# Both layer normalisations of a Mamba-like layer with a mixture of experts, applied by ScalarE instead of VectorE

## The reference

```python
def _layernorm(x, axis=-1, eps=1e-05):
    m = jnp.mean(x, axis=axis, keepdims=True)
    v = jnp.var(x, axis=axis, keepdims=True)
    return (x - m) / jnp.sqrt(v + eps)

x = L0_attn_x
x = x + _L0_attn_ref(_layernorm(x), ...)   # projections, conv of 4 taps, damped oscillator per head, gate, output
x = x + _L0_ffn_ref(_layernorm(x), ...)    # router over 8 experts, the best 2, GELU experts, a shared expert
```

## Time and profile before

| | us |
|---|---|
| median of 3 runs | 580.45 |
| lowest and highest run | 577.06, 587.46 |
| the profiled execution | 578.51 |
| its span, from the first to the last instruction | 576.8 |

### The profile page before, as it was taken

The page is one execution under the profiler, slowest core; times in us unless marked ns, Lnnn a source line. Parts: engine busy times, 40 slices in busy tenths (PEclk is TensorE's granted clock), DMA queues, the critical chain, the costliest instruction groups (busy, mean ns, idle before and its releaser), DMA issues.

```text
span 576.8 us, 9365 instructions
## 1 busy us (share of the span) xinstructions
PE 435.0 (75%) x3240; PEld 352.0 (61%) x3240; DVE 486.3 (84%) x1206; ACT 275.1 (48%) x459; POOL 208.7 (36%) x269
## 2 busy tenths in 40 slices
PE   2942006997889929897989928897889929986997
PEld 1832005886756717785856717786756718875886
DVE  5389998989899998989799998979899997886342
ACT  1641233555646623455665624455646624334363
POOL 2021006767630007667620007657630007784000
PEclk9977557999989977999999969999989978999999
DMA  7400000000000010000000000000000000000000
GB/s 232 125 1 1 0 0 1 2 3 1 1 1 0 2 36 2 1 1 1 2 1 1 2 18 0 3 2 0 1 2 0 1 19 2 2 2 1 1 9 11
DMA packets 8433, 7.05 MB, mean 12 GB/s; under 512 B 1593, under 2 KB 7618, under 8 KB 8258
## 3 DMA queue, kind: packets, MB, share of 16 engines
q1 hardware_dynamic: 8386, 6.46, 3.7%
HBM read 5.41 MB, written 1.05 MB: 11 GB/s over the span
## 4 chain that ended last, share of the span: by engine, by line
DVE 24%; PE 22%; POOL 12%; issue 8%; ACT 3%; DVEq 0%; POOLq 0%; ACTq 0%
POOL vt L1493 4%; PE HB L514 4%; DVE tp L1102 3%; POOL big L1490 3%; DVE xr L1319 3%; PE HB L522 3%; DVE mm L1219 2%; PE RR L542 2%; PE OO L542 2%; DVE mm L1181 2%; DVE hist L1102 2%; POOL rinv L1510 2%; DVE pr L1181 2%; PE GV L542 2%; PE BC L560 1%
## 5 line engine op out<-in xcount | busy, mean ns | idle before, releaser
L1490 POOL TENSOR_TENSOR big<-mm 128x256 f32<-128x256 f32 x64 | 48.8, 763 | 258.1 <-DVE mm L1219 258.1
L560 PE MATMUL BC<-xnT,winT 128*128 128x128 f32 x512 | 76.4, 296 | 79.8 <-DVE mm L1219 79.7
L560 PEld LDWEIGHTS BC<-xnT,winT 128*128 128x128 f32 x512 | 67.6, 206 | 85.7 <-DVE mm L1219 82.2
L1493 POOL TENSOR_TENSOR vt<-mm 128x256 f32<-128x256 f32 x64 | 59.3, 927 | 0.0
L823 ACT ACTIVATE pr<-hist 128x512 f32<-128x512 f32 x32 | 34.0, 1115 | 52.2 <-DVE hist L1102 52.2
L514 PE MATMUL HB<-xnT,w 128*128 128x512 f32 x108 | 54.5, 631 | 2.5 <-ACT sqs L908 2.1
L845 ACT ACTIVATE big<-GV 128x256 f32<-128x256 f32 x64 | 24.6, 384 | 66.5 <-PE GV L584 65.5
L582 PE MATMUL GV<-big,vt 128*128 128x128 f32 x256 | 44.6, 299 | 11.6 <-POOL vt L1493 11.6
L1102 DVE TENSOR_TENSOR tp<-big,hist 128x256 f32<-128x256 f32 x124 | 51.8, 418 | 1.4
L1217 DVE TENSOR_TENSOR mm<-BC,pr 128x512 f32<-128x512 f32 x64 | 44.1, 688 | 4.9
L582 PEld LDWEIGHTS GV<-big,vt 128*128 128x128 f32 x256 | 36.0, 203 | 18.4 <-POOL vt L1493 15.9
(11 more groups left out here) (188 smaller groups left out, 1075.7 us busy)
## 6 DMA issues: line engine op xcount, KB each, us to landing
xr<-in_x SPq DMA_DIRECT2D x4, 256.0 KB, 4.8
winT<-in_w_inT SPq DMA_DIRECT2D x1, 1024.0 KB, 6.3
w<-in_rw SPq DMA_DIRECT2D x1, 1024.0 KB
out<-xr SPq DMA_DIRECT2D x3, 256.0 KB, 2.3
taps<-in_dw_wT SPq DMA_DIRECT2D x1, 512.0 KB, 3.7
w<-in_sw SPq DMA_DIRECT2D x2, 128.0 KB
out<-xr SPq DMA_DIRECT2D x2, 128.0 KB, 1.8
winT<-in_w_inT SPq DMA_DIRECT2D x1, 130.0 KB, 2.8
```

The source lines that it names most:

```text
L560: last = pe.matmul(b[:, j * TS:(j + 1) * TS], winT[:, col:col + NS], xt, start=True, stop=True)
L1490: pool.tensor_tensor(wt[q % 8][:], m[:, 0], m[:, 3], ALU.add)
L1493: pool.tensor_tensor(vt[q % 2][:], view(m, 5 * TS, (-3 * TS, 2), (1, TS)), view(m, 3 * TS, (TS, 2), (1, TS)), ALU.subtract).then_inc(wv_do ...
```

## The change

ScalarE applies both normalisations as Identity(scale * x + bias), with rstd as per-partition scale and a new tile `shift` = -mean * rstd as per-partition bias. VectorE makes `nmean` = -mean, one instruction more in each `norm_stats`; GpSimd makes `shift` from it after rstd, behind a wait of its own chain, and signals `ln_rstd` only then. `norm_apply` moves to ScalarE's queue: at the head behind the exponential of the parameters; LN1 in step 2, behind that step's `vt_copy`; LN2 behind the z of the next group and ahead of `norm2`; EARLY in step 15; LAST ahead of its `norm2`. Two waits are added for order that VectorE's queue gave before: `norm_stats` waits for the `ln_rstd` of the normalisation before it, and TensorE's first expert output of a whole group waits for the state sum of the group's last tile (`z_done`), since both use the bank RR.

```diff
@@ tensor, expert_out
+                if whole(u) and e == 0:
+                    pe.wait_ge(z_done, GT * (u + 1))
@@ scalar
+            def norm_apply(kind, u):
+                g, c0, c1 = UNITS[u] if kind == LN2 else (u, 0, GT)
+                n = ln_index(kind, u)
+                act.wait_ge(ln_rstd, n + 1)
...
+                if n:
+                    act.wait_ge(h_ready, USE[last] + 1)
+                for c in range(c0, c1):
+                    last = act.activation(xn[:, c, :], xr[g % 3][:, c, :], ACT.Identity, bias=shift[:, c:c + 1],
+                                          scale=rstd[:, c:c + 1])
+                last.then_inc(ln_xn, 1)
...
             act.activation(sgt[:, 2 * NH:4 * NH], sgt[:, 0:2 * NH], ACT.Exp, scale=-1.0).then_inc(prep_a, 1)
+            norm_apply(LN1, 0)
...
                     if g + 1 < NG:
+                        if k == F_XN:
+                            norm_apply(LN1, g + 1)
                         front_early(g + 1, k - 1)
...
                     else:
+                        if k == A_XN:
+                            norm_apply(LN2, EARLY)
...
                     front_late(g + 1, "z", 1)
+                    norm_apply(LN2, g)
                     norm2(g)
...
+            norm_apply(LN2, LAST)
             norm2(LAST)
@@ vector
+                if ln_index(kind, u):
+                    dve.wait_ge(ln_rstd, ln_index(kind, u))
                 for c in range(c0, c1):
                     last = dve.bn_aggr(mv[:, c, :], stats[:, c, :])
                 link(last)
+                dve.tensor_scalar(nmean[:, c0:c1], mv[:, c0:c1, 0], -1.0, None, ALU.mult)
                 dve.tensor_scalar(mv[:, c0:c1, 1], mv[:, c0:c1, 1], EPS_LN, None, ALU.add).then_inc(ln_var, 1)
-            def norm_apply(kind, u):
...
-                for c in range(c0, c1):
-                    last = dve.tensor_scalar(xn[:, c, :], xg[:, c, :], mv[:, c, 0:1], rstd[:, c:c + 1],
-                                             ALU.subtract, ALU.mult)
-                last.then_inc(ln_xn, 1)
...
                     matrices(g + 1, 0)
-                    norm_apply(LN2, g)
                     matrices(g + 1, 1)
@@ gpsimd, rstd_of
-                pool.tensor_tensor(rstd[:, c0:c1], mv[:, c0:c1, 1], mhalf[:, c0:c1], ALU.pow).then_inc(ln_rstd, 1)
+                link(pool.tensor_tensor(rstd[:, c0:c1], mv[:, c0:c1, 1], mhalf[:, c0:c1], ALU.pow))
+                pool.tensor_tensor(shift[:, c0:c1], nmean[:, c0:c1], rstd[:, c0:c1], ALU.mult).then_inc(ln_rstd, 1)
```

More of the change, by code:

```diff
@@ L143, in build @@
         rstd = sb("rstd", 128, GT)
+        shift = sb("shift", 128, GT)
+        nmean = sb("nmean", 128, GT)
         dtts = [sb(f"dtt{i}", 128, KP) for i in range(2)]
@@ L748, in _ @@
             by_tile = lambda t: t.rearrange("p (c t) -> p c t", c=GT)
+            def norm_apply(kind, u):
+                g, c0, c1 = UNITS[u] if kind == LN2 else (u, 0, GT)
+                n = ln_index(kind, u)
+                act.wait_ge(ln_rstd, n + 1)
+                if kind == LN2:
+                    last = ("xnT", u + 1) if whole(u) else ("xnT2", u - 1)
+                else:
+                    last = ("xnT2", g - 2) if g >= 2 else ("xnT", g - 1)
+                if n:
[4 more added lines that the diff above has]
+                last.then_inc(ln_xn, 1)
             def front_early(g, k):
@@ L1037, in front_early @@
                     norm_stats(LN1, g)
-                if k == F_XN:
-                    norm_apply(LN1, g)
                 if k == F_EXP:
@@ L1359, in _ @@
             dve.wait_ge(prep, 1)
-            front_early(0, F_XN)
             dve.wait_ge(ld_u, LD_U)
@@ L1411, in _ @@
                             norm_stats(LN2, EARLY)
-                        if k == A_XN:
-                            norm_apply(LN2, EARLY)
                         if k == A_ROUTER + 1:
@@ L1433, in _ @@
                     matrices(g + 1, 2)
-            norm_apply(LN2, LAST)
             for e in range(MID_STEPS - A_ADDS, NE - 1):
```

## The result

The changed kernel takes 587.75 us, median of 4 runs (586.04 to 589.87); the kernel before, over the same runs, 579.48 (577.06 to 587.46). The ratio is 1.0157, with a 95% interval of 1.0111 to 1.0202: slower by 1.1 to 2.0%, at the border of what this kernel's measurement tells from no change. The profiled execution took 588.24 us, its span 586.5, 9.7 more than before; mean granted clock 0.900 (before 0.911). In the program after, the rows are L767, shift L1469, nmean L1047, the added eps L1048, the square L860, z L829, the pair's first product L1212, the transposes L438, the router's product L501.

A forecast was written before the change was run, and what follows sets the result against it. VectorE was busiest (84%), but the normalised rows stood on the chain that ended last. LN1 1.6 + LN2 3.6 + head 0.6 + halves 0.1 and 0.8 = +6.7 us on 578.51: 585.2, median 586.0; own range 582 to 590, overall 579 to 593.

The forecast's parts named there:

- ScalarE's instruction: Each new 128-column normalising instruction on ScalarE: 0.48 us alone, one every 0.38 us in a row.
- shift: GpSimd's added tiny multiplication behind rstd: ScalarE is released 0.28 us after rstd.
- LN1: Three sites early in the groups: next pair's square queues behind the normalisation, 0.54 us each, +1.6 us.
- VectorE's relief counts: Rival: ScalarE's queue holds nothing wanted, so VectorE's freed time at LN1 and LN2 is won; about -12, 566 us; chance 0.07.
- LN2: Three sites between groups: rows behind z's copy on ScalarE make TensorE's transposes 1.19 us late each, +3.6 us.
- the third rival: At six LN1 and LN2 sites TensorE's clock falls to the 1.2 GHz level; 10 us on top, 595.4; chance 0.13.
- its sign for the third rival: Behind LN1 and LN2 sites: a granted clock below 0.95 would mean the third rival holds.
- Head: Start of the kernel: TensorE begins the transposes at 8.45 in place of 7.84, +0.6 us.
- Second half: Last group's second half: normalisation behind expert 7's GELU on ScalarE delays TensorE's transposes, +0.8 us.
- First half: Last group's first half: shift fits GpSimd's 0.55 us idle time or hangs out by up to 0.1, +0.1 us.
- Costed at nothing: Nine negated means on VectorE (1.8 us if uncovered), TensorE's new wait for the last state sum, and activation table loads: 0.
- Absorbed: Rival: delays inside groups go into VectorE's idle time; only head and second half remain, +1.4, 580.0; chance 0.14.

The follow-up runs named there:

- experiment 1: `ln1_later`: changed kernel with LN1's normalisation one step later in ScalarE's queue and its TensorE transposes a step later too; 583.38 us, ratio 1.0105.
- Experiments 6 and 7: Experiment 6 is `ln1_none`, ratio 0.9973; experiment 7 is `only_ln1_spread`, ratio 0.9974.
- `only_ln1_spread`: Kernel before with only LN1 of groups 1 to 3 on ScalarE, two rows behind each of two pairs; 577.6 us, ratio 0.9974.
- `rows_back_no_nmean`: Changed kernel with all 32 normalising instructions back on VectorE and the negated mean dropped, shift still made but unread; 579.86 us, one run.
- `ln1_none`: Kernel before with LN1 rows of groups 1 to 3 left out, ScalarE writing one column instead; negated mean and shift stay; 578.79 us, ratio 0.9973.

## Why the prediction was right, and where it was off

The range of 582 to 590 around the forecast of 586.0 holds the measured 587.75, and the result is a slower kernel within the border of 2%. The order in ScalarE's queue costs what was forecast, place by place. That the total fits as well as it does is in part luck: in the profile 6.7 us were forecast and 9.7 came, two terms were too small, and the 0.8 us added for the median rest on the three runs' 580.45, where later medians of the kernel before were 578.7 to 579.3. By its steps:

- *ScalarE's instruction*, 0.48 us and one per 0.38: measured 0.482, and 1.64 for four. *shift* 0.28 us behind rstd's end: 226.24 to 226.55, 0.31.
- *LN1*, 0.54 a site behind the square: 0.55 to 0.59, three times, in both profiles of the changed kernel. Shown by experiment 1, where the wait went with the order. The prediction was wrong about its premise, though: it held VectorE's 3.3 us at the site for the most that could be won, and against "VectorE's relief counts" it named only ScalarE's order. Experiments 6 and 7 show that with the order mended some 0.45 us a site is won and the other 2.8 are not there: the pairs behind wait for other engines' work.
- *LN2*, 1.19 a site: right where the clock holds (1.15 on the average of `ln1_later`'s three), but 2.0 and 2.3 on average in the two profiles of the changed kernel. The term is short by the router's product at the low clock and what follows it, 2.5 us over three sites in the first profile, 3.4 in the second. This is the mechanism of the third rival, which was given 0.13 as a case of its own with 10 us; it came as an addition of a few. The argument against it, that TensorE kept 1.00 around one hole of 1.80, was a single stretch, and it ends 0.36 us behind that hole; the trace has 1.00 from 274 to 280 us too, but the same rows showed 0.79 behind the other hole. What the prediction did not look at is the seam itself: in the kernel before the clock was already 0.66 behind two of the three LN2 sites. So its sign for the third rival, a clock below 0.95 there, was met (0.79 and 0.54) and could not tell: it holds without the change too. What counts is whether the fall comes ahead of the router's product.
- *Head* 0.6: 0.65, and 0.58 to 0.80 in the other profiles with it. *Second half* 0.8: 0.8 to 1.0 where the clock behind the last pair is as in the kernel before, and gone when the rows stand ahead of the GELU.
- *First half* 0.1: 0.62. The term looked only at whether shift fits into GpSimd's idle time. What cost was nmean, "costed at nothing" at LN1 and LN2 and not looked at here: it pushed the adding of eps behind the start of a 256-column sum of GpSimd.
- *Costed at nothing.* TensorE's new wait and the activation table: nothing in any trace. The negated means: nothing at LN1, as forecast (0.23, 0.26 and 0.24 with, 0.24, 0.26 and 0.24 without), but 0.16 at the head (0.30 with, 0.14 without, one profile each) and 0.6 at the first half, so 0.8 us.
- *Absorbed*, the rival at 0.14: no step of the table is taken back inside a group, but for the two stray stretches.

Added up, 0.65 + 1.70 + 3 x 1.19 + 0.62 + 0.8 = 7.3 us of order, near the predicted 6.7, and 2.5 of clock. The stray stretches cancel, which is luck: the profile of before has one in the pairs of group 2, that of after one in group 1. Of the eleven others, the changed kernel's second profile has one in group 2, `only_ln1_spread` and `rows_back_no_nmean` have one in group 1, `ln1_none` has low clock in both, and seven have none there. What starts them is open.

The Trainium skill, "SBUF — State Buffer", section "SBUF: two separate sides", describes an exclusive lock on a pair of ports between GpSimd and those VectorE instructions that run in a two-port mode or have two inputs out of SBUF: who comes second waits for the whole instruction of the first. The adding of eps, 0.17 us there without nmean and 0.71 from 527.66 on with it, ends at 528.37 behind a sum that ends at 528.34, which agrees with that; no row shows in which mode it ran. The Trainium skill's "TensorE: Matmul & The Clock Gate", section "What's actually happening", has the clock follow how busy TensorE has been, by a monitor that runs free of the kernel's start. The traces agree in that the third site's product took 1.22 us in one execution of the changed kernel and 1.88 in the other; no run here shows the cause.

## What to carry to other kernels

Before work is taken from the busiest engine, ask what the others do meanwhile. The time that VectorE spends at one place of a software pipeline may be the time in which the loop's other engines catch up. A version that simply leaves the work out tells the most that can be won (here half a microsecond of 3.3 a site). Work given to an in-order queue belongs behind the instruction that someone already waits for, and a longer hole of TensorE at a serial seam should be priced at its length and, as a chance, at up to about a microsecond more for the products right behind it. Look at the granted clock of the same seam before the change first: here it was low there already, at no cost. A tiny instruction added ahead of another can push that one beside a large one of GpSimd.

## What was unexpected in the hardware

The granted clock fell behind the seam between two groups in every kernel, with the short hole of TensorE too: over the 5 us behind the router's eight small products it was 0.66 to 0.71 at 13 of 18 sites with a TensorE hole of 1.0 to 1.2 us, and 0.50 to 0.74 at all 21 with one of 1.6 to 2.2 us. With the longer hole it often fell ahead of or inside the products, which took 1.22 to 1.88 us in place of 1.06 at 15 of 21 sites; with the short hole they took over 1.2 us at 1 of 18. And VectorE's addition of eps took 0.17 us or 0.70, depending on whether it started 0.03 us ahead of GpSimd's sum or 0.04 behind its start.
